# A decoder kernel on one core: work reordered at the two borders of the second attention, and one load of masks moved in the SyncE queue

## The reference

```python
x = x + L0_attn(layernorm(x))          # causal linear attention, 16 heads of 64, phi = elu + 1
x = x + L0_xattn(layernorm(x), ctx)    # attention over ctx (16, 375, 256), masked keys, 16 heads of 16
x = x + L0_ffn(layernorm(x))           # causal attention with RMS norms of q and k, then a mixture of 4 experts
x = x + L1_attn(layernorm(x))          # causal attention through a rank of 64
x = x + L1_xattn(layernorm(x), ctx)    # attention over the last 65 keys, with rotary positions
x = x + L1_ffn(layernorm(x))           # quantised rows times ternary weights

# the two that the change touches
energy = einsum('nqhd,nkhd->nhqk', q, k); energy = where(mask == 0, -1e20, energy)
attn = softmax(energy / sqrt(256)); out = einsum('nhqk,nkhd->nqhd', attn, v)
num = q . sum(k v); den = q . sum(k); out = num / (den + 1e-6)      # the first attention
```

## Time and profile before

| | |
|---|---|
| median of 3 runs | 1312.16 us (1310.6 to 1314.02) |
| the profiled execution | 1310.68 us, of which the profile's span is 1308.9 us |
| PE busy | 1249.4 us, 95% of the span |
| DVE, ACT, POOL busy | 734.5 us, 503.4 us, 281.9 us |
| chain of work that ended last | PE 90%, issue 2%, DVE 2%, ACT 2%, DMA 1% |
| mean granted PE clock | 0.991 |

### The profile page before, as it was taken

The page is one execution under the profiler, slowest core; times in us unless marked ns, Lnnn a source line. Parts: engine busy times, 40 slices in busy tenths (PEclk is TensorE's granted clock), DMA queues, the critical chain, the costliest instruction groups (busy, mean ns, idle before and its releaser), DMA issues.

```text
span 1308.9 us, 34635 instructions
## 1 busy us (share of the span) xinstructions
PE 1249.4 (95%) x14031; PEld 970.5 (74%) x14031; DVE 734.5 (56%) x1730; ACT 503.4 (38%) x1075; POOL 281.9 (22%) x382
## 2 busy tenths in 40 slices
PE   7999999998999999889999999999999899999995
PEld 5788777774676766557767889999998667777764
DVE  5666666665567666478864211111112666789985
ACT  2111111110555555456657333323332444444444
POOL 2000000101211211588844000000001000234532
PEclk9999999997999999999999999999999999999999
DMA  7212111110422221012200200000000000000001
GB/s 223 63 45 47 42 31 33 33 29 21 92 62 60 67 52 39 7 47 81 72 16 21 51 1 0 0 3 0 0 1 1 3 6 4 15 18 18 18 7 58
DMA packets 48480, 45.38 MB, mean 35 GB/s; under 512 B 15408, under 2 KB 44896, under 8 KB 48336
## 3 DMA queue, kind: packets, MB, share of 16 engines
q1 hardware_dynamic: 48336, 43.33, 12.7%
HBM read 39.44 MB, written 2.78 MB: 32 GB/s over the span
## 4 chain that ended last, share of the span: by engine, by line
PE 90%; issue 2%; DVE 2%; ACT 2%; DMA 1%; POOL 1%; SPq 1%; ACTq 0%; DVEq 0%
PE banks L322 51%; PE banks L826 6%; PE banks L804 4%; PE banks L985 3%; PE banks L998 3%; PE banks L315 3%; PE banks L1045 3%; PE banks L842 3%; PE banks L959 2%; PE banks L657 2%; PE banks L615 2%; PE banks L1024 2%; ACT area L1559 1%; PE banks L1040 1%; PE banks L894 1%
## 5 line engine op out<-in xcount | busy, mean ns | idle before, releaser
L1840 DVE TENSOR_REDUCE Y_room<-banks 112x2 f32<-112x750 f32 x128 | 114.2, 935 | 49.3 <-PE banks L804 49.1
L1989 DVE TENSOR_REDUCE area<-banks 112x8 f32<-112x896 f32 x96 | 100.1, 1085 | 56.3 <-PE banks L985 56.3
L1559 ACT ACTIVATE area<-banks 112x896 f32<-112x896 f32 x96 | 82.8, 914 | 111.5 <-PE banks L1045 111.5
L322 PE MATMUL banks<-room,area 128*112 128x256 f32 (+1 forms) x384 | 121.1, 467 | 3.2 <-issue 2.8
L2121 DVE SCALAR_TENSOR_TENSOR X<-banks,area,X 128x192 f32 (+1 forms) x56 | 23.3, 418 | 160.4 <-PE banks L322 160.1
L1637 ACT ACTIVATE room<-banks 128x256 f32<-128x256 f32 x123 | 47.2, 384 | 166.0 <-PE banks L322 165.9
L1446 ACT ACTIVATE area<-banks,Y_room 125x896 f32<-125x896 f32 x96 | 90.2, 1010 | 37.8 <-PE banks L826 32.9
L322 PE MATMUL banks<-area,room 128*128 128x224 f32 x512 | 103.5, 362 | 0.6 <-ACT area L1403 0.6
L322 PEld LDWEIGHTS banks<-area,room 128*128 128x128 f32 x512 | 97.8, 194 | 3.3 <-ACT area L1403 1.0
L322 PE MATMUL banks<-room,l 128*128 128x256 f32 x448 | 99.5, 379 | 0.0
L322 PEld LDWEIGHTS banks<-room,area 128*112 128x112 f32 x384 | 68.1, 183 | 40.6 <-issue 27.2
(11 more groups left out here) (237 smaller groups left out, 2417.2 us busy)
## 6 DMA issues: line engine op xcount, KB each, us to landing
area<-den_scratch SPq DMA_DIRECT2D x32, 224.0 KB, 3.6
Y_room<-in_ctx SPq DMA_DIRECT2D x16, 375.0 KB
area<-in_ctxT SPq DMA_DIRECT2D x64, 93.8 KB
area<-area SPq DMA_DIRECT2D x192, 2.6 KB
l<-in_l SPq DMA_DIRECT2D x2, 1024.0 KB, 5.4
room<-in_ctxT SPq DMA_DIRECT2D x16, 112.0 KB, 2.2
out<-X SPq DMA_DIRECT2D x16, 112.0 KB, 1.9
X<-in_x SPq DMA_DIRECT2D x1, 1568.0 KB, 17.3
```

What stands on the lines that cost most here:

```text
L322: last = nc.tensor.matmul(dst, a, w, start=(k == 0), stop=(k == len(lhs) - 1))
L1559: a_.activation(c_pT[:, i * 8 * S:(i + 1) * 8 * S].rearrange("p (j n) -> p j n", j=2), banks[0:S, 2 + 2 * i:4 + 2 * i, 0:4 * S], ACT.Exp). ...
L1840: v_.tensor_reduce(b_nb[u][:, 4 * a + k:4 * a + k + H + 1:H], banks[0:S, 2 * x:2 * x + 2, 0:SC], AX_X, ALU.max, negate=True).then_inc(Bs[" ...
L1989: v_.tensor_reduce(c_nb[:, 8 * i:8 * i + 8].rearrange("q (j n) -> q j n", j=2), banks[0:S, 2 + 2 * i:4 + 2 * i, 0:4 * S].rearrange("q j (n ...
```

## The change

Nothing is added to or taken from what is computed, and every engine issues the same instructions. These move:

- PE, first border: the column sums become a function of their own, `sums_a`. Of batch 15 they and `scores_b(0, 0)` now stand ahead of `output_a(14)`. In the turns of the first attention the sums stay where they are, and only the semaphores on which they wait change (bank 6 read, instead of the batch before normalised).
- DVE, first border: the last two triangular products stand ahead of `normalised(14)`; `denominators(15)` behind it and ahead of `highest(0, 0)`; `residual_a(14)` behind `highest(0, 1)`.
- SP: the load of `blocks_all` goes from ahead of the contexts of batches 2 and 3 to the end of step 4 of `ctx_loads`. In its place SP waits until the rows of `maxima_rows(0)` have landed.
- Second border: on PE the projections of batches 0, 1 and 2 each stand earlier by a piece. On ACT `squares_c(0)`, `columns_c(1)` and `squares_c(1)`, `columns_c(2)` stand ahead of the exponentials that they stood behind. On DVE the norm and sums of `variance_c(2)`, `sums_c(0)`, `row_c(2)`, `stats_c(3)` stand ahead of `phase_b(B, ...)`, and `sums_c(1)` ahead of the wait for the last weighted values.

```diff
@@ SP
             maxima_rows(0)
             sp.wait_ge(pre["ctx2"].sem, 1)
-            sp.dma_start(blocks_all, T["consts"][:, C_END:C_END + C_WORDS]).then_inc(ld["mask"].sem, 16)
+            sp.wait_ge(Bs["mr"].sem, Bs["mr"].at(64))
             for n in range(2, 4):
                 context(n, n)
@@ SP, ctx_loads
                     values(b + 1, (w + 1) % 2)
+                if b == QUAD:
+                    sp.dma_start(blocks_all, T["consts"][:, C_END:C_END + C_WORDS]).then_inc(ld["mask"].sem, 16)
@@ PE
-            def weighted_a(b):
+            def sums_a(b):
                 pe.wait_ge(A["sm"].sem, A["sm"].at(4 * b + 4))
-                pe.wait_ge(A["nm"].sem, A["nm"].at(2 * b))
-                pe.wait_ge(A["pj"].sem, A["pj"].at(12 * (b // 2) + 10 + 2 * (b % 2)))
+                pe.wait_ge(A["den"].sem, A["den"].at(b))
...
                 last.then_inc(A["ds"].sem, 1)
+            def weighted_a(b):
+                pe.wait_ge(A["nm"].sem, A["nm"].at(2 * b))
+                pe.wait_ge(A["pj"].sem, A["pj"].at(12 * (b // 2) + 10 + 2 * (b % 2)))
                 for m in range(8):
@@ PE, phase_a
                     output_a(2 * p - 2)
+                    sums_a(2 * p - 1)
                     weighted_a(2 * p - 1)
...
                     output_a(2 * p - 1)
+                sums_a(2 * p)
                 weighted_a(2 * p)
@@ PE, first border
-            output_a(B - 2)
             pe.wait_ge(pre["masks"].sem, 1)
             scores_b(0, 0, 0, 0)
+            sums_a(B - 1)
+            output_a(B - 2)
             weighted_a(B - 1)
@@ PE, second_to_third
                 weighted(n - 1, 3, (n - 1) % 2)
+                attention(0, B, -3, -2)
                 turned(n, 0, n % 4)
...
                 turned(n, 3, n % 4)
-                attention(0, B, -3, -2)
+                attention(0, B, -2, -1)
                 sums_t(n - 1)
...
                 output_t(n - 1)
-                attention(0, B, -2, -1)
+                project_qk(2)
                 for t in range(4):
                     weighted(n, t, n % 2)
                 output_b(n - 1)
                 sums_t(n)
-                project_qk(2)
@@ ACT, second_to_third
                 sums_b(n - 1)
+                squares_c(0)
+                columns_c(1)
                 for t in range(4):
                     weights(n, t, n % 2)
-                squares_c(0)
-                columns_c(1)
+                squares_c(1)
+                columns_c(2)
                 weights(n, 4, n % 2)
                 weights(n, 5, n % 2)
                 results_b(n - 1)
-                squares_c(1)
-                columns_c(2)
@@ DVE, last turn of phase_a
+                masked(1, 2)
+                masked(1, 3)
                 if not more:
                     normalised(2 * p)
-                masked(1, 2)
-                masked(1, 3)
+                    denominators(2 * p + 1)
@@ DVE, first border
-            residual_a(B - 2)
             highest(0, 0, 0)
             highest(0, 1, 0)
-            denominators(B - 1)
+            residual_a(B - 2)
@@ DVE, second_to_third
                 first_rows(1)
-                phase_b(B, 0, B // 2)
                 variance_c(2)
                 sums_c(0)
                 row_c(2)
                 stats_c(3)
+                phase_b(B, 0, B // 2)
+                sums_c(1)
                 variance_c(3)
                 dve.wait_ge(Bs["pv"].sem, Bs["pv"].at(2 * B))
                 normed_c(0)
-                sums_c(1)
```

## The result

| | before | changed | ratio, 95% interval |
|---|---|---|---|
| median of the runs beside each other | 1312.98 us (1310.6 to 1314.02, 4 runs) | 1298.63 us (1297.54 to 1301.37, 4 runs) | 0.9896 (0.9874 to 0.9917) |
| the same, later | 1311.54 us (11 runs) | 1301.25 us (1297.32 to 1301.9, 6 runs) | 0.991 (0.9891 to 0.9928) |
| the profiled execution, span | 1308.9 us | 1295.8 us | |

The kernel is faster by 14.35 us in the first comparison and by 10.3 us in the second; 10.0 us were forecast. Between the two profiled executions the span differs by 13.1 us. PE's busy time fell from 1249.4 to 1245.3 us with the same instructions: in this pair 4.1 us are the same work done at the higher clock. That part is not steady: in another profiled execution of the changed kernel, further down, PE is busy 1249.5 us.

What follows compares the result with a forecast made beforehand. PE, busy 95% of the span, was taken as the bound, so only its stalls and low clock could be won. 1.8 plus 3.5 plus 4.7 is 10.0 us: 1302.2 us by the median, range 1297.5 to 1308 us.

Steps and rivals of the forecast that it cites:

- The bound: Whole kernel: PE bounds it, busy 95% of the span; steady stretches behind each border keep what the border gains.
- First border, 1.8 us: Start of the second attention: scores and sums fill PE's hole of 2.83 us ahead of `output_a(14)`, gaining 1.8 us.
- the upper bound of 3.5: First border: gain of 3.5 us if the clock stays at 2.4 GHz through `output_a(14)`.
- the case that the sum assumed: First border: the clock still falls, `output_a(14)` takes 5.36 us, and the gain is 1.8 us.
- Masks, 3.5 us: PE's wait for batch 1's maxima rows: 1.9 us off the 2.5 us stall, plus 1.6 us of half clock.
- The estimate by the Trainium skill's rule: Masks' move: rows stay behind the values load on five engines, so it buys 1.3 us, not 1.9.
- Second border, 4.7 us: Second to third attention: POOL's large power starts 6.8 us earlier and leaves the chain; `to_columns(0)` comes 4.7 us earlier.
- No new wait: Sign: no new wait in step 4 or 5 of the second attention; a wait for batch 15's exponential would be wrong.
- The rival by which ACT or DVE hold PE at a new place: Second border wins only 1.7 us and the masks nothing: 3.5 us in all, 1308.7 us; chance 0.07.
- The slower rival: Second border: short pieces with gaps drop PE's clock to 1.2 GHz into the third attention, 1316 us; chance 0.03.
- Masks nothing: The masks did not hold the maxima rows; stall and half clock stay, 1305.7 us; chance 0.17.
- The clock does not fall at the first border: The hole there is half as long, so the clock holds: 1.7 us more, 1300.5 us; chance 0.17.

Runs made afterwards that it cites:

- sums0_late: The changed kernel with `sums_c(0)` on DVE put back behind `phase_b(B)`, the rest of the second border as changed: 1302.31 us, ratio 0.9927.
- qk2_late: The changed kernel with `project_qk(2)` on PE put back behind `sums_t` of batch 15: 1299.57 us, ratio 0.9898.
- no_b1: The changed kernel without the first border's part, so masks and second border only: 1300.37 us, ratio 0.9918 to the kernel before.
- b1_only: The kernel before with only the first border's edits on PE and DVE: 1311.32 us against 1312.62 us, ratio 0.9992.
- masks_only: The kernel before with only the masks' load moved to step 4, with the new wait for the first maxima rows: 1306.16 us, ratio 0.9947.
- hole_busy: The kernel before with 12 unused matmuls put into the hole ahead of `output_a(14)`: 1310.38 us, ratio 0.9978.

## Why the prediction was right, step by step

- **The bound.** It held: the steady stretches gave back and took nothing (124.89 of 130 us before and after, −0.1 us from `to_columns(0)` to the end). But that −0.1 is one pair. The stretch behind `to_columns(0)` takes 752.9 to 757.3 us over all profiled executions, 752.9 to 754.7 of them in kernels without the edit of the second border, so a difference of a few microseconds between two executions need not come from an edit.
- **First border, 1.8 us.** In the profiled pair it was 3.8 us, above the upper bound of 3.5. The filling was worth what was forecast up to the second scores (some 1.6 us), but the clock stayed at `output_a(14)` in both executions of the changed kernel, in the one with this border alone and in the three with matmuls put in (3.64 us each time), and fell in `sums0_late` and `qk2_late`, which have the changed kernel's instructions there, with 5.32 us in both and a gain of 1.0 us. The clock is the failed assumption, and it is one of the execution and not of the order alone. Why the two executions lost it wasn't settled. They are also the case that the sum assumed, and there the forecast 1.8 us were 1.0: the sum lets everything behind the second scores run as before, and the later half clock was longer. The piece is itself unsteady: 36.82 to 37.90 us in the six executions with the old order. By the medians the part is worth 1 to 3 us on top of the others (`no_b1`), and 1.3 us alone, within the noise.
- **Masks, 3.5 us.** Mechanism right, size off: this is the step of the sum that was too small. In the profiled pair it gave 3.9 us, where the stall of 2.5 us and the clock's 1.6 us would be 4.1: all of the stall went, and not 1.9 of it. The piece from the first `turned` to the weighted values is 196.12 to 196.28 us in all nine executions profiled with the masks moved. With the masks in front and the values load whole it is 199.78, 200.01 and 201.50 us in three kernels that have the same order there, so the price of the stall is in part luck of the execution, 3.7 to 5.4 us, and the profile of before had a cheap one; `b1_only` has 6.2 us. By the medians the move is worth 6.5 us alone, and 5.4 on top of the second border (0.9918 against 0.9959). The scatter of the stall goes some way to explain 6.5, whose interval begins at 5.2, and not all of it. The estimate by the Trainium skill's rule (DMA: Bandwidth & Descriptors) left 1.2 us of stall, because the rows stay behind the values load. They do stay behind it, and that load ends 1.3 us earlier against the first `turned` in `masks_only`, as by that estimate. But the rows land 2.4 us earlier (15.61 to 13.21 us), because they follow more closely and land sooner after their last packet, and no stall was left: on the size of the gain the measurement decides against the estimate.
- **Second border, 4.7 us.** 4.6 us in the profile and 5.3 us by the medians. The border takes 24.09 or 24.10 us in all five executions with exactly these edits, and 27.26 to 29.75 us in the five without. POOL's power came 6.9 us earlier (6.8 forecast), the hops were 2.4 us (2.5), and `sums0_late` shows that the sums' place on DVE carries 2.4 us of it.
- **No new wait.** None in step 4 or 5, and none of a batch 15 exponential. The rival by which ACT or DVE hold PE at a new place did not come about. The slower rival did in a small way: the changed kernel's clock falls behind the border, from 545.6 to 549.0 us in the first profile and from 544.3 to 551.1 us in the second, and comes back by itself. The kernel before had its fall inside the border (550.8 to 554.3 us).
- **The rivals.** "Masks nothing" fell with `masks_only`. "The clock does not fall at the first border" is what six of eight executions of the changed kernel's border show, three of them with matmuls put in. The forecast of 10.0 us lies below the 13.1 of the profiled pair by what the clock (1.7), the masks (0.4) and the unforecast pieces (0.9 ahead of the border, and the shorter half clock) gave. That the second median came within 1 us of the forecast is luck in part: some 3 us of the 3.5 us between the two profiles of the changed kernel lie in stretches of which the forecast says nothing.

## What to carry to other kernels

A stall behind a queue of loads has no fixed price: read it in more than one execution before it goes into a sum, since one profiled execution may show the cheap case. In this kernel small DMAs on which an engine waits belonged ahead of large ones, and a load that kept only a third of the DMA engines busy cost twice, in its own time and in that of the rows behind it. An edit measured alone in front of such a wait can look like nothing (`b1_only`, ratio 0.9992), so take the wait away before you judge it.

## What was unexpected of the hardware

- The same matmuls in the same order ran at 2.4 GHz in one execution and at 1.2 GHz in another. With 1.3 us of idling in front of the scores, `output_a(14)` took 3.64 us in three executions and 5.32 us in two. With matmuls put into the gap it took 3.64 to 3.71 us in all four, and behind the old order's gap of 2.7 to 3.3 us 5.09 to 5.37 us in all five. The Trainium skill (TensorE: Matmul & The Clock Gate, "What's actually happening") states that the chip's watch over PE's activity does not start with the kernel, so that the point of a change depends on the run; these executions fit that and do not prove it.
- A piece of some 10 us at a granted clock of 0.50, with PE busy 9.66 of 10 us, stands behind the first border in every execution profiled, and matmuls put in ahead did not remove it. In `sums0_late`, `qk2_late` and `hole_busy` it lasts over 13 us. It holds scores of 18 rows and 375 columns and `output_a(15)`. Its cause stays open.
- Four small transfers issued within 2.2 us landed 9.1 us after the first issue with the masks, two contexts and a values load in front of them (`b1_only`), and 4.7 us after it without the masks (`masks_only`).
